# Cross-attention and an eight-expert FFN on one core: vectors turned to columns by one transpose, x statistics by pairs, two late pairs

## What is computed

```python
h      = layernorm(x)
normed = rmsnorm(h) * norm_w
v_pool = concat([normed, ctx], axis=1)                 # 128 own rows, 128 of the context
q, k   = normed @ q_w.T, v_pool @ k_w.T
attn   = softmax(where(causal_or_ctx, q @ k.T / 16, -inf))
alpha  = sigmoid(h @ gate_w.T + gate_b)
x2     = x + (1 - alpha) * h + alpha * (attn @ v_pool)
xn     = layernorm(x2)                                 # 2048 token rows
for e in range(8):                                     # 512 listed tokens each
    y = gelu(xn[top_idx[:, e]] @ W1[e] + b1[e]) @ W2[e] + b2[e]
    out[top_idx[:, e]] += y * combine_weights[top_idx[:, e], e]
out += x2
```

## Time and profile before

| | us |
|---|---|
| median of 3 runs (lowest, highest) | 274.85 (274.27, 275.41) |
| the profiled execution, whole | 275.01 |
| its span | 273.2 |
| PE busy | 263.7 |
| DVE busy | 218.4 |
| ACT busy | 188.2 |
| POOL busy | 156.9 |

### The profile page before, as it was taken

One profiled execution on the slowest core, in us unless ns is written; L12 is line 12 of the kernel. 1 busy time (PEld: TensorE's weight loads), 2 busy tenths in 40 slices (PEclk: granted clock), 3 DMA queues, 4 the chain that ended last, 5 costly groups with the idle time before them and its releaser, 6 DMA issues.

```text
span 273.2 us, 5127 instructions
## 1 busy us (share of the span) xinstructions
PE 263.7 (97%) x1477; PEld 225.8 (83%) x1477; DVE 218.4 (80%) x553; ACT 188.2 (69%) x349; POOL 156.9 (57%) x152
## 2 busy tenths in 40 slices
PE   7899999999989999999999999999999999999993
PEld 3688899999876888888888888888888888888983
DVE  1899999899985779968878896796887889689453
ACT  2687899887666975786676587668657758773540
POOL 4349765565768717656456466655645656514525
PEclk9999999999999999999999999999999999999998
DMA  5986257588446945454464544645446561210211
GB/s 154 341 232 199 94 154 200 148 231 270 133 149 150 388 154 157 129 169 155 134 208 154 156 142 135 168 118 207 160 138 180 160 181 56 59 35 34 65 49 69
DMA packets 30560, 42.44 MB, mean 155 GB/s; under 512 B 5521, under 2 KB 24283, under 8 KB 30416
## 3 DMA queue, kind: packets, MB, share of 16 engines
q1 hardware_dynamic: 25120, 29.74, 35.0%
q0 software_dynamic: 4608, 12.24, 15.4%
q10 hardware_dynamic: 816, 0.26, 0.4%
HBM read 33.54 MB, written 9.24 MB: 157 GB/s over the span
## 4 chain that ended last, share of the span: by engine, by line
PE 81%; DVE 6%; issue 4%; DMA 4%; POOL 1%; ACT 1%; SPq 0%; DVEq 0%; POOLq 0%
PE bank L1423 19%; PE bank L1202 12%; PE bank L1203 12%; PE bank L1204 12%; PE bank L1424 10%; PE bank L1250 4%; PE bank L1294 3%; DMA x_all<-in_x_dram 2%; PE bank L1351 2%; DMA x_all<-token_rows,idx_all 2%; PE bank L1370 1%; PE bank L1371 1%; PE bank L1374 1%; PE bank L1318 1%; POOL out_dram L557 1%
## 5 line engine op out<-in xcount | busy, mean ns | idle before, releaser
L752 ACT ACTIVATE keysT<-bank,biasT 128x512 f32<-128x512 f32 x63 | 43.6, 692 | 55.6 <-PE bank L1204 39.3
L557 POOL DMA_INDIRECT out_dram<-h,sidx x32 | 36.7, 1146 | 40.2 <-DVE h L1094 34.8
L547 POOL DMA_INDIRECT x_all<-out_dram,idx_all x32 | 36.6, 1143 | 23.6 <-DMA out_dram<-h,sidx 16.0
L1202 PE MATMUL bank<-x_hi,w_parts 128*128 128x512 f32 (+1 forms) x114 | 45.1, 396 | 0.0
L1203 PE MATMUL bank<-x_lo,w_parts 128*128 128x512 f32 (+1 forms) x114 | 44.4, 389 | 0.0
L1204 PE MATMUL bank<-x_hi,w_parts 128*128 128x512 f32 (+1 forms) x114 | 44.1, 387 | 0.0
L1119 DVE TENSOR_TENSOR g_lo<-keysT,g_hi 128x512 fp32r<-128x512 f32 x32 | 22.1, 692 | 27.0 <-ACT g_hi L753 26.3
L543 POOL DMA_INDIRECT x_all<-token_rows,idx_all x28 | 30.7, 1095 | 18.9 <-DVE factor L1143 12.4
L1423 PE MATMUL bank<-w_parts,g_hi 128*128 128x512 f32 x112 | 40.5, 396 | 0.0
L1124 DVE TENSOR_TENSOR w_parts<-w_raw,w_parts 128x512 fp32r<-128x512 f32 x56 | 38.4, 686 | 0.0
L758 ACT CAST w_parts<-w_raw 128x512 fp32r<-128x512 f32 x56 | 34.9, 623 | 0.0
(11 more groups left out here) (187 smaller groups left out, 681.5 us busy)
## 6 DMA issues: line engine op xcount, KB each, us to landing
w_raw<-in_L_ffn_W_dram SPq DMA_DIRECT2D x32, 512.0 KB
idx_rows<-in_L_ffn_top_idx_dram SPq DMA_DIRECT2D x8, 256.0 KB, 4.1
out_dram<-x SPq DMA_DIRECT2D x8, 256.0 KB, 2.9
hn_cnat<-in_ctx_dram SPq DMA_DIRECT2D x7, 256.0 KB, 2.8
token_rows<-xn SPq DMA_DIRECT2D x7, 256.0 KB, 2.2
hn_cnat<-in_L_ffn_b_dram SPq DMA_DIRECT2D x1, 1024.0 KB
x_all<-in_x_dram SPq DMA_DIRECT2D x3, 256.0 KB, 6.8
x_all<-in_x_dram SPq DMA_DIRECT2D x1, 768.0 KB, 9.4
```

Source lines behind the costliest of these rows:

```text
L547: g.indirect_dma_start(accg[:, t, :], None, flat, list_of(e, t)).then_inc(acc_in[t], 16)
L557: g.indirect_dma_start(flat, idx(sidx[:, t:t + 1].bitcast(U32), 0), newrow[:, t, :], None, bounds_check=N - 1, oob_is_err=False).then_inc( ...
L752: a.activation(g32[:, f % NG, :], ps_up[f % 2][:, :], ACT.Gelu_apprx_tanh, bias=bias)
L1202: t_.matmul(dst, lhs_hi, rhs_hi, start=first, stop=False)
```

## The change

- norm_w and gate_b are loaded as 4 rows of 128 into `vec_rows`; PE turns them to columns with one transpose, ACT copies them (`cols_rdy`). The spread of the two vectors over all partitions stands ahead of the first hn transposes. SP loads context 0 ahead of x batches 2-3. The first query runs its passes over the high part first and waits for the low part after.
- Statistics of x and their powers are made pair by pair: 0-5 in setup, 6-9 in pair 0, 10-11, 12-13 and 14-15 in pairs 1, 2 and 3. `hn_rows(1)` is on DVE, no longer ACT. DVE's loop is written out.
- Two late pairs in place of three; the table's zeros and the one-hots shrink to 4 batches. PE first writes zeros into the two banks, then adds gathered and late rows as they come.
- In the last pair the probabilities are transposed, evacuated and multiplied by halves. In pair 6 the query evacuation and `normalised_x2(5)` go ahead of the tanh. POOL's gathers of the first rows are split around the powers of the last pairs. Chunks 2 and 3 of expert 1's weights are loaded after b2.

Core of the diff:

```diff
-    EARLY_PAIRS = NPAIR - 3
+    EARLY_PAIRS = NPAIR - 2
...
+        late_hi = [gateT_hi[:, :, :], hnT_hi[:, 0, :, :]]
+        late_lo = [gateT_lo[:, :, :], hnT_lo[:, 0, :, :]]
...
+        ps_pT_last = [banks[6][:, 0:H].rearrange("p (j s) -> p j s", j=2),
+                      banks[1][:, 0:H].rearrange("p (j s) -> p j s", j=2)]
         ps_pv_last = [banks[7][:, 0:H], banks[4][:, 0:H]]
         ps_list = banks[6]
+        ps_cols = banks[6][:, 0:2 * KH]
...
             load_x(0, 0, 2)
             load_weight(0, q_w, wts_in)
+            load_ctx(0)
             load_x(1, 2, 4)
-            load_ctx(0)
...
-                    for late in (LAST - 2, LAST - 1):
-                        sp.wait_ge(xn_rdy, 2 * late + 2)
-                        sp.dma_start(rows_v[:, 2 * late:2 * late + 2, 0:H], xn2[:, late % 2, :, :])\
-                            .then_inc(xn_out[late % 2], 16)
+                    sp.wait_ge(xn_rdy, 2 * r + 2)
+                    sp.dma_start(rows_v[:, 2 * r:2 * r + 2, 0:H], xn2[:, r % 2, :, :]).then_inc(xn_out[r % 2], 16)
...
-                if r % 2 == 1:
+                if r in (1, 3):
                     sp.wait_ge(wlo0_rdy, r + 1)
                     load_chunk(1, r // 2)
             sp.wait_ge(pv_mm, NPAIR)
             row_broadcast(b2_bc, b2.rearrange("e h -> (e h)")).then_inc(b2_in, 16)
+            for c in range(2, NCH):
+                sp.wait_ge(wlo0_rdy, 2 * c + 2)
+                load_chunk(1, c)
...
             x_powers(0, 2, 1)
             x_powers(2, 4, 2)
-            hn_shifts(2, 4, 2)
+            pool.wait_ge(bc_rdy, 1)
+            pool.wait_ge(hn_rdy, 4)
+            normed_rows(0, 0)
             x_powers(4, 6, 3)
             hn_shifts(4, 6, 3)
-            pool.wait_ge(bc_rdy, 1)
-            normed_rows(0, 0)
-            x_powers(6, 10, 4)
-            hn_shifts(6, 10, 4)
...
                     pool.wait_ge(shift_rdy, p - 1)
                 g.tensor_tensor(x_plus_h[:, s, :], x_all[:, ds(p * (2 * H), 2 * H)],
                                 h[:, s, :, :].rearrange("p b h -> p (b h)"), ALU.add).then_inc(xh_rdy, 1)
+                if p == 1:
+                    x_powers(8, 10, 5)
+                    hn_shifts(8, 10, 5)
+                if 2 <= p < NPAIR // 2 + 1:
+                    x_powers(2 * p + 6, 2 * p + 8, p + 4)
+                    hn_shifts(2 * p + 6, 2 * p + 8, p + 4)
                 if is_last(p):
-                    gather_first_rows(range(NT - 1))
+                    expert0_lo(LAST - 2)
+                    gather_first_rows(range(2))
...
-                    x_powers(10, NB, 5)
-                    hn_shifts(10, NB, 5)
+                    x_powers(6, 8, 4)
+                    hn_shifts(6, 8, 4)
                 else:
-                    if not is_last(p):
+                    if not is_last(p) and not is_last_but_one(p):
                         expert0_lo(p - 1)
                     rstd(p - 1, 1 - s)
                 if is_last(p):
-                    gather_first_rows(range(NT - 1, NT))
+                    gather_first_rows(range(2, NT - 1))
...
+            last_rstd(0)
+            gather_first_rows(range(NT - 1, NT))
+            last_rstd(1)
...
+            act.dma_start(vec_rows[0:KH, :], norm_w.rearrange("(k p) -> k p", p=P)).then_inc(vec_in, 16)
+            act.dma_start(vec_rows[KH:2 * KH, :], gate_b.rearrange("(k p) -> k p", p=P)).then_inc(vec_in, 16)
...
+            act.wait_ge(cols_mm, 1)
+            a.copy(norm_w_gate_bT[:, :, :].rearrange("p n k -> p (n k)"), ps_cols).then_inc(cols_rdy, 1)
...
-                if is_last(p):
-                    act.wait_ge(xn_rdy, 2 * p - 2)
-                    act.wait_ge(q_mm, NPAIR)
-                    a.copy(late_hi[0], xn2[:, s, :, :]).then_inc(late_hi_rdy, 1)
...
+                    if is_first(p) and b == 0:
+                        hn_transposed(1, 1)
...
+                if is_last(p):
+                    for b in range(2):
+                        act.wait_ge(last_pT_mm, b + 1)
+                        a.copy(probsT[:, b, :, :], ps_pT_last[b]).then_inc(last_pT_ev, 1)
...
+                if is_last_but_one(p):
+                    query(p + 1)
+                    normalised_x2(p - 1, 1 - s, use - 1)
...
+            act.wait_ge(cols_rdy, 1)
...
+            act.wait_ge(bc_mm, 1)
+            a.copy(vec_bc[:, :], banks[7][:, :]).then_inc(bc_rdy, 1)
...
-            x_sums(2, 3, 1)
-            dve.wait_ge(nwT_in, 16)
+            dve.wait_ge(cols_rdy, 1)
             M_low(0)
             M_low(1)
             hnT_low(0, 0)
-            x_sums(3, 4, 1)
+            x_sums(2, 4, 1)
             x_aggregates(2, 4)
             x_variances(2, 4)
             x_stats(4, 6, 2)
             x_variances(4, 6)
-            h_rows(0, 0, False)
-            x_rms(0, 4, 2)
-            x_sums(6, 8, 3)
...
+                else:
+                    dve.wait_ge(pow_rdy, 2)
+                    hn_rows(1, 1)
+                    gateT_low()
                 for b in range(2):
-                    if is_first(p) and b == 1:
-                        gateT_low()
...
+                if p == 1:
+                    hnT_low(2, 0)
...
+                    if is_last_but_one(p):
+                        stats2(p - 1, 1 - s)
+                        aggr2(p - 1, 1 - s)
...
+                    x_rms(0, 4, 2)
+                    h_rows(0, 0, False)
...
+                    x_sums(6, 10, 3)
...
+                    x_variances(6, 8)
+                    x_variances(8, 10)
...
+                if p == 1:
+                    aggr2(p - 1, 1 - s)
+                    x_stats(10, 12, 4)
+                    x_variances(10, 12)
+                    x_rms(4, 10, 5)
...
+                if is_last_but_one(p):
+                    shift(p - 1, 1 - s)
+                elif p > 1:
                     aggr2(p - 1, 1 - s)
-                    if not is_last(p):
-                        h_rows(p + 1, 1 - s)
+                if p in (2, 3):
+                    x_stats(2 * p + 8, 2 * p + 10, 4)
+                    x_variances(2 * p + 8, 2 * p + 10)
+                if p == LAST - 3:
+                    x_rms(10, NB, 8)
+                if not is_first(p) and not is_last(p):
+                    dve.wait_ge(pow_rdy, p + 2)
+                    h_rows(p + 1, 1 - s)
...
-                    dve.wait_ge(late_hi_rdy, 1)
-                    dve.wait_ge(xn_rdy, 2 * LAST - 2)
-                    v.tensor_tensor(late_lo[0], xn2[:, s, :, :], late_hi[0].bitcast(F32), ALU.subtract)\
-                        .then_inc(late_lo_rdy, 1)
...
+
+            for p in range(NPAIR):
+                attention(p, p % 2, p // 2)
...
-            keep_warm(10)
+            keep_warm(9)
+            pe.wait_ge(ident_rdy, 2)
+            pe.wait_ge(vec_in, 32)
+            t_.transpose(ps_cols, vec_rows[:, :], ident[0:2 * KH, 0:2 * KH]).then_inc(cols_mm, 1)
+            keep_warm(1)
...
-            hn_transposes(0, 0)
-            pe.wait_ge(nwT_in, 16)
-            pe.wait_ge(gate_b_in, 16)
+            pe.wait_ge(cols_rdy, 1)
             for n in range(2):
                 for k in range(KH):
                     last = t_.transpose(banks[7][:, (n * KH + k) * P:(n * KH + k + 1) * P],
                                         norm_w_gate_bT[:, n, k:k + 1].broadcast_to([P, P]), ident[:, :])
             last.then_inc(bc_mm, 1)
+            hn_transposes(0, 0)
             context_transposes(0, 0, 0)
             pe.wait_ge(setup_lo, 2)
-            query(0, 0)
+            pe.wait_ge(hnT_hi_rdy, 1)
+            for m in range(KH):
+                c = slice(m * P, (m + 1) * P)
+                for k in range(KH):
+                    t_.matmul(ps_q[:, m, :], M_hi[:, k, c], hnT_hi[:, 0, k, :], start=(k == 0), stop=False)
+                    t_.matmul(ps_q[:, m, :], M_lo[:, k, c], hnT_hi[:, 0, k, :], start=False, stop=False)
+                pe.wait_ge(hnT_lo_rdy, 1)
+                for k in range(KH):
+                    last = t_.matmul(ps_q[:, m, :], M_hi[:, k, c], hnT_lo[:, 0, k, :], start=False, stop=(k == KH - 1))
+            last.then_inc(q_mm, 1)
...
+                    if is_last(p) and b == 0:
+                        last_probs_transposed(0)
...
+                if is_last(p):
+                    last_probs_transposed(1)
...
-                if is_first(p):
-                    hn_transposes(2, 0)
-                if is_last(p):
-                    pe.wait_ge(log_rdy, 2 * NPAIR - 1)
-                    pe.wait_ge(late_hi_rdy, 1)
-                    for b in range(2):
-                        late_rows(0, b, late_hi, first=b == 0)
...
-            early_rows(range(1))
+            pe.wait_ge(log_rdy, 2 * NPAIR - 1)
+            for k in range(KH):
+                t_.matmul(ps_xT[k][:, :], junk[:, 0:P], junk[:, :], start=True, stop=False)
+            early_rows(range(2))
+            pe.wait_ge(late_hi_rdy, 1)
+            for b in range(2):
+                late_rows(0, b, late_hi)
```

(23 more changed lines are left out.)

125 lines of the change are left out of this document (51 added, 74 removed).

## The result

| | before | changed |
|---|---|---|
| median of 11 runs (lowest, highest), us | 274.85 (274.27, 275.41) | 275.78 (275.46, 276.35) |
| ratio to before, 95% interval | | 1.0038 (1.0029 to 1.0048) |
| the profiled execution, whole | 275.01 | 275.61 |
| its span | 273.2 | 273.8 |

The change makes the kernel slower by 0.9 us (0.4%) where 1.75 less was forecast. By the bound named in the prediction (about 0.5%) that is no change; the interval excludes 1 all the same.

What follows compares the result with a forecast made beforehand. PE, busy nine tenths or more of almost every slice, was taken as the bound. Terms -1.2 - 1.3 + 1.35 - 0.6 = -1.75 took 275.01 to 273.26 us (273.1 on the median's scale); own range 272.2 to 274.1, 8-in-10 range 271.6 to 274.9.

Steps and rivals of the forecast that it cites:

- lists and weights, taken 0: Late list load and expert 1's weight chunks: SP's issue moves up less than PE, still covered; 0 us, bound +0.4.
- from 84 us on all shifts as it is: After the passage into expert 0, everything keeps its length and moves with the summed gain of 1.75 us.
- Setup, -1.2.: Start of the kernel: M and the first query come earlier, pair 0's logits near 11.65; 1.2 us less.
- Pairs 0 and 1, -1.3.: First two pairs: DVE loses statistics and its stall at pair 0's residual; 1.3 us less, bounds 0 and -1.3.
- Pairs 2 to 4, +1.35.: Statistics return to DVE, PE waits ahead of the transposed probabilities; 1.35 us more, bounds +0.7 and +1.9.
- Into expert 0, -0.6.: Pair 7's logits to first up product: a late pair's low part leaves DVE's chain; 0.6 us less.
- three signs of being wrong: Pair 7's logits move under 0.5 or over 2.2 us; their way to up product does not shrink; experts 0-7 change length.
- 3: Into expert 0: PE stands about 1.7 us, its clock falls to half; +3 to +4, about 276.7 us; chance 0.05.
- Rival 1: Pairs: DVE takes back everything won, setup's gain is waited away too; about 274.3 us; chance 0.18.
- Rival 2: Pairs: DVE keeps up, give-back only 0.3, setup -1.4; -3.0, about 271.9 us; chance 0.16.
- rival 5: Setup is not shortened because the vectors' rows land late and PE waits ahead of M; about 274.0 us; chance 0.08.
- Rival 4: Pairs: four added powers on POOL hold DVE off; up to +3.4, about 276.5 us; chance 0.03.

Runs made afterwards that it cites:

- changed_again: The changed kernel, unaltered, timed once more on one chip with two other versions: 275.71 us, ratio 1.0042 to the kernel before.
- list_early_fill: Changed kernel with the last eighth of the rows' list loaded in pair 5 and two products of zeros in PE's second stand: 274.37 us, ratio 0.9986.
- vec_columns: list_early_fill with norm_w and gate_b loaded column by column, without PE's transposition: 275.79 us, ratio 1.0040 to the kernel before.
- stats_early: list_early_fill with the statistics of pairs 5 to 7 back on DVE in pair 0: 274.37 us, ratio 1.0006 to the kernel before.
- before_b2_early: Kernel before with only SP's queue reordered: b2 right behind the list, chunks 2 and 3 of expert 1 behind b2: 275.27 us, ratio 1.0022.
- list_early: Changed kernel with the last eighth of the rows' list loaded in pair 5, no filling products: 275.44 us, ratio 1.0012 to the kernel before.
- both_again: list_early_fill timed once more, on one chip with two other versions: 274.31 us, ratio 0.9991 to the kernel before.
- fill_second: Changed kernel with two products of zeros in PE's second, shorter stand only: 275.86 us, ratio 1.0036 to the kernel before.
- b2_behind: Changed kernel with two filling products, the list left late, b2 and the chunks held back until it landed: 277.02 us, ratio 1.0082.
- gather_ahead: list_early_fill with the fourth gather of the first rows right behind the third: 275.69 us, ratio 1.0036 to the kernel before.
- hi_direct: list_early with ACT rounding pair 6's rows for PE straight from the residual, no filling products: 274.30 us, ratio 0.9990.

## Why the prediction was wrong

The step that failed is **lists and weights, taken 0**, and with it "from 84 us on all shifts as it is". It looked at when SP issues the list and how much cover ACT leaves, and found "Bound +0.4". It did not count what the change puts beside the list in the same breath: 1 MB of b2, 0.5 us behind it instead of 4.4, and 512 KB of chunk 2. I costed chunk 2 by its own reader only, and b2 not at all. The list then took 5.6 us instead of 3.7, landed at 87.7, and set ACT's second gelus at 88.8 whatever came before. From the first up product to PE's last product the kernel before takes 185.5 us; changed_again takes 186.9, and list_early_fill 185.6. With the list early and the clock held the kernel is at 274.3 to 274.4; the step is worth 1.4 us. It is the largest part of the miss and not all of it: forecast and measurement lie 2.7 us apart, and two other terms below were mis-sized by 1.1 together.

The other steps, with what they measured:

- *Setup, -1.2.* -1.09 at pair 0's logits (11.79, forecast 11.65), and carried whole, as vec_columns shows. Right within the spread of the start; M began 0.30 earlier (5.72), not 0.5.
- *Pairs 0 and 1, -1.3.* -1.41, a tenth past the bound, which I had set at the value itself; 20.38 and 28.16 against 20.3 and 28.1, the stall at the residual gone. Right.
- *Pairs 2 to 4, +1.35.* +1.89 by pair 7's logits. The profile calls 0.89, 0.16 and 0.16 idle ahead of the transposed probabilities, but it counts from the modelled end of the product before. From start to start, logits to transposed probabilities, pairs 2 to 4 take 5.16, 4.44 and 4.46 us where they took 4.11, 4.11 and 4.10: 1.74 us of waits, where 1.2 was forecast. What comes after them is the 0.15 forecast. Mis-sized by 0.5, at the bound.
- *Into expert 0, -0.6.* Of it -0.52 came, up to the last pair's first half (73.98). But "everything from 75.11 to 83.51 keeps its length", 8.40 us, was 8.90 (73.96 to 82.86 in list_early_fill). Behind the last pair's first high part PE now has the fourth gathered tile (0.37 us), and two products of the second bank (0.47) now stand ahead of ACT's first copy, since the last products go over both banks in turn; that these are the reason is argued from PE's order, not tried.

Together -1.09 - 1.41 + 1.89 - 0.52 + 0.50 = -0.63 at the first up product, where list_early_fill has -0.65. So the pairs and the passage together cost 0.5 us, where 0.55 less was forecast, and on balance the setup alone wins. The list adds 1.4 from there to the second gelus: changed_again is 0.78 early at the first up product (82.73), 0.62 late at the second gelus, and 0.5 late in its span.

Of the three signs of being wrong that the prediction names, pair 7's logits moved by 0.61 us, just inside. At full clock the way from them to the up product hardly shrank (14.87 us in changed_again, 14.89 before), and in the first profile it grew to 16.26. Experts 0 to 7 kept their length in the first profile only because the clock's fall had made them start late; in changed_again they are 1.4 us longer.

Of the rivals, 3 happened and is not the answer. Its condition was wrong (it was to decide once PE's stand reached the 2 us of the end; with stands of 1.43 and 0.48 us it fell in some executions, and in changed_again's profile it stayed at 1.00 through the 4.1 us without a product at the end), and its price was too high (1.8, not 3 to 4), and most of that was covered. Rival 1 is half true: DVE takes back in full what it wins in the pairs (1.89 against 1.41), and stats_early shows the spread of the statistics to win nothing, but setup's gain is not waited away. Rival 2 fell with the 1.89, rival 5 with M at 5.72. Rival 4 did not show: the mix of pair 1 (32.80, 0.69 us) ran at its usual length beside a power on POOL (32.26, 1.03 us). The rule of the Trainium skill (SBUF — State Buffer, "SBUF: two separate sides") is narrower than I put it: a DVE operation with two inputs in SBUF is held only against a GpSimd operation that reads SBUF. The powers do read it, so the rule would still have the mix wait; it did not, and the measurement decides. But DVE's `var_eps` at 27.03 took 0.91 us where it takes 0.17, beside POOL's `expert0_lo`; a long tensor operation still holds it.

## What to carry to other kernels

When a change moves a bulk load, cost it by the transfers that are in flight beside it, not only by its own reader: find the small load with the nearest deadline and ask what will share the engines with it. When a profile shows a striking cause, take that cause away before believing it; here the clock's fall and the late list ended within a tenth of a microsecond of each other, and the cure of either alone brought nothing sure. A load whose buffer is free long before belongs at the point where it comes free.

## What the runs showed of the hardware

- A load was slowed by loads issued behind it on the same queue. The list (256 KB) took 3.7 us with b2 coming 4.4 us later, 4.1 with b2 held back until it had landed, and 5.6 with 1 MB of b2 0.5 us behind it and 512 KB of weights 0.5 us behind that, in before_b2_early as in the changed kernel. Whether it would be so from another queue, no run shows. The Trainium skill (DMA: Bandwidth & Descriptors, "Queues, rings and completion order") says that descriptors of one queue are consumed in ring order on each DMA engine, but that a later one may finish its write before an earlier one. So the order of issue need not shield a load from what follows it. The list agrees: 1.5 us more with the loads behind it than without.
- The granted clock fell in some executions of one and the same kernel and not in others: in 7 of 18 of the changed kernel and 6 of 12 of list_early, whose profiles have stands of PE of 1.43 and 0.48 us and of 1.80 us within 74 to 77.6 us. With two filling products behind the first gathered rows it fell in none of 24 executions of list_early_fill and both_again, though the longest stand was as long as ever (1.54 us), nor in the 5 of fill_second. But the two products are no safeguard: with them in place mean clocks of 0.990 to 0.994 stand in 3 of 12 executions of stats_early, 5 of 12 of b2_behind, 1 of 9 of vec_columns and 1 of 5 of gather_ahead, and where in the kernel the clock fell there is not known, since the profiled executions were others. hi_direct, without such products, has none in 11. In the first profile it was at the lower level from 77.3 to 80.8 us, with PE busy throughout.
- Behind the last product the clock falls in some executions and not in others, over the same 4.1 us without a product: its mean there is 0.76 in both_again's profile and 1.00 in changed_again's. Mean clocks of 0.996 and 1.000 of these two differ by that alone; both have 1.00 up to the last product.
- In the faster versions some executions with a mean clock of exactly 1.000 stand 0.7 us above those at 0.996 to 0.999 (both_again: 274.94 to 275.08 against 274.09 to 274.44). I have no cause for it.
